# A layer kernel whose SyncE queue, norm rows, statistics and scales stand at other places of a step

## What is computed

```python
    x = L0_attn_x
    x = x + _L0_attn_ref(_layernorm(x, axis=-1), L0_attn_Wq, L0_attn_Wk, L0_attn_Wv, L0_attn_Wu, L0_attn_bu)
    x = x + _L0_ffn_ref(_layernorm(x, axis=-1), L0_ffn_W_r, L0_ffn_W_k, L0_ffn_W_v, L0_ffn_mu_r, L0_ffn_mu_k)
...
        dot = jnp.einsum('bhqd,bhkd->bhqk', q, k) / jnp.sqrt(jnp.float32(s))
        att = jax.nn.softmax(dot, axis=-1)
        out = jnp.einsum('bhqk,bhkd->bhqd', att, v)
        out = out.transpose(0, 2, 1, 3).reshape(b, t, h * s)
        return out @ Wu.T + bu
...
            xr = mu_r * x + (1.0 - mu_r) * x_prev
            xk = mu_k * x + (1.0 - mu_k) * x_prev
            r = jax.nn.sigmoid(jnp.einsum('btc,dc->btd', xr, W_r))
            k = jnp.einsum('btc,dc->btd', xk, W_k)
            k_act = jnp.square(jax.nn.relu(k))
            out = r * jnp.einsum('btc,dc->btd', k_act, W_v)
```

## Time and profile before

| | |
|---|---|
| median of 3 runs | 2272.7 us (2272.09 to 2285.43) |
| profiled execution, its own time | 2274.27 us |
| its span | 2272.4 us |
| mean granted TensorE clock | 0.972 |
| PE busy | 2114.4 us, 93% |
| DVE busy | 1872.0 us, 82% |
| ACT busy | 1645.5 us, 72% |
| POOL busy | 1514.8 us, 67% |

### The profile page before, as it was taken

The page is one execution under the profiler, slowest core; times in us unless marked ns, Lnnn a source line. Parts: engine busy times, 40 slices in busy tenths (PEclk is TensorE's granted clock), DMA queues, the critical chain, the costliest instruction groups (busy, mean ns, idle before and its releaser), DMA issues.

```text
span 2272.4 us, 39598 instructions
## 1 busy us (share of the span) xinstructions
PE 2114.4 (93%) x13084; PEld 1085.5 (48%) x13084; DVE 1872.0 (82%) x3598; ACT 1645.5 (72%) x3137; POOL 1514.8 (67%) x1568
## 2 busy tenths in 40 slices
PE   4999999999999999999999999999999999999985
PEld 3445444445454445444444544444445445454433
DVE  5788888878888888888888888888888888888762
ACT  2477777777877777777777777777777777777663
POOL 5347766667866676776676786666777667677335
PEclk8799999999999999999999999999999999999887
DMA  6544455544455553445564445555444556443410
GB/s 153 117 109 106 95 101 120 130 108 106 96 109 111 129 125 99 103 94 110 130 129 110 104 94 110 111 129 120 104 105 95 106 131 130 106 103 88 83 29 23
DMA packets 133467, 242.09 MB, mean 107 GB/s; under 512 B 24849, under 2 KB 79761, under 8 KB 120977
## 3 DMA queue, kind: packets, MB, share of 16 engines
q1 hardware_dynamic: 133264, 239.56, 47.5%
HBM read 136.71 MB, written 83.89 MB: 97 GB/s over the span
## 4 chain that ended last, share of the span: by engine, by line
PE 46%; POOL 18%; issue 15%; ACT 7%; DVE 5%; SPq 5%; DMA 4%; POOLq 0%; ACTq 0%; DVEq 0%
PE d_ps L957 19%; PE st_ps L895 12%; PE pv_ps L927 11%; PE s_ps L913 4%; SPq L314 4%; POOL parts L431 3%; DMA attnT<-attn 3%; DVE mx L707 3%; POOL xrT L440 3%; ACT yn L581 2%; ACT probs L666 2%; POOL f_lo L454 2%; POOL sums L482 2%; POOL rope_t L413 2%; POOL rope_t L416 2%
## 5 line engine op out<-in xcount | busy, mean ns | idle before, releaser
L707 DVE TENSOR_REDUCE mx<-s_ps 128x1 f32<-128x512 f32 x2048 | 1336.6, 678 | 300.9 <-PE s_ps L913 300.5
L666 ACT ACTIVATE probs<-st_ps 128x512 f32<-128x512 f32 x2048 | 1155.7, 597 | 484.9 <-PE st_ps L895 465.5
L895 PE MATMUL st_ps<-q_st,k_st 50*128 50x512 f32 x2048 | 813.3, 461 | 92.3 <-ACT probs L666 50.7
L913 PE MATMUL s_ps<-k_st,q_st 48*128 48x512 f32 x2048 | 815.8, 465 | 7.8 <-DMA k_st<-parts_scratch 5.4
L895 PEld LDWEIGHTS st_ps<-q_st,k_st 50*128 50x128 f32 x2048 | 323.2, 187 | 717.3 <-ACT probs L666 485.1
L927 PE MATMUL pv_ps<-probs,v_ext 128*32 128x512 f32 x4096 | 551.0, 610 | 0.0
L913 PEld LDWEIGHTS s_ps<-k_st,q_st 48*128 48x128 f32 x2048 | 322.6, 187 | 19.1 <-DVE mx L707 10.4
L482 POOL TENSOR_TENSOR sums<-sums,inv 128x256 f32<-128x256 f32 x128 | 93.0, 727 | 305.5 <-DVE inv L734 305.5
L461 POOL TENSOR_TENSOR f_lo<-yn,f_hi 128x512 fp32r<-128x512 f32 x128 | 166.6, 1312 | 44.8 <-ACT f_hi L631 44.7
L927 PEld LDWEIGHTS pv_ps<-probs,v_ext 128*32 128x32 f32 x4096 | 81.1, 108 | 179.1 <-issue 171.3
L431 POOL TENSOR_TENSOR parts<-parts 128x1024 fp32r<-128x1024 f32 x62 | 148.1, 2388 | 19.4 <-ACT parts L596 19.4
(11 more groups left out here) (116 smaller groups left out, 4007.2 us busy)
## 6 DMA issues: line engine op xcount, KB each, us to landing
parts_scratch<-parts SPq DMA_DIRECT2D x64, 1024.0 KB, 4.5
q_st<-parts_scratch SPq DMA_DIRECT2D x128, 256.0 KB, 5.4
k_st<-parts_scratch SPq DMA_DIRECT2D x128, 256.0 KB, 6.3
xn<-in_L_attn_x_dram SPq DMA_DIRECT2D x32, 512.0 KB, 9.2
q_st<-parts_scratch SPq DMA_DIRECT2D x128, 128.0 KB, 6.8
k_st<-parts_scratch SPq DMA_DIRECT2D x128, 128.0 KB, 7.3
attnT<-attn SPq DMA_DIRECT2D x512, 32.0 KB, 2.0
y<-in_L_attn_x_dram SPq DMA_DIRECT2D x32, 512.0 KB, 7.0
```

The source lines that it names most:

```text
L666: nc.scalar.activation(probs[:, u % SLOTS, j, :], st_ps[:, n % 2, :], ACT.Exp, scale=float(D) ** -0.5).then_inc(exp_done, 1)
L707: nc.vector.tensor_reduce(mx[:, col:col + 1], s_ps[:, ring_bank(n), :], AX.X, ALU.max).then_inc(max_done, 1)
L895: nc.tensor.matmul(st_ps[:, n % 2, :], k_st[par][row:row + SROWS + MROWS, slot, c * P:(c + 1) * P], q_st[par][row:row + SROWS + MROWS, slo ...
L913: nc.tensor.matmul(s_ps[:, ring_bank(n), :], q_st[at][row:row + SROWS, slot, qc * P:(qc + 1) * P], k_st[at][row:row + SROWS, slot, :], sta ...
```

## The change

**SyncE.** The 1 MB store of the second half of sequence b+1 stood first in the step; now the four moves of the attention result and the four of the maxima of group 1 stand before it.

**ScalarE.** The two chunks of `norm2` that ran together are made singly: at (6, 0), (6, 1), (7, 0), (7, 2) in place of two at (6, 0) and two at (7, 2). `norm1` of chunks 0 and 1 moves from (0, 0), (0, 2) of a step to (15, 0), (15, 2) of the step before (so its sequence is b+3 there), and chunks 2 and 3 from (2, 0), (2, 1) to (0, 0), (0, 2).

**VectorE.** In unit 5 the statistics of chunks 0 and 1 stand ahead of the transpose out of `pv_ps`, with both stages at place 0; the transpose and the reciprocal move to place 1. Those of chunks 2 and 3 move from (6, 1), (6, 2) to (5, 3), (6, 0).

**GpSimd.** The second norm's first `scales` stands ahead of `divide(b, 0)`. The first norm's second `scales` stands between the two pairs of rotary products of K, where it stood behind the rotary sums.

```diff
@@ SyncE's step @@
-                store_parts(b.plus(1), 1 - par, 1)
                 move_attn(b.plus(-1), 3)
                 move_max(b, 1)
+                store_parts(b.plus(1), 1 - par, 1)
                 store_out()
                 load_stacks(0)
                 load_x()
@@ GpSimd's step @@
                 low_a(1)
+                scales(b.plus(-1), 0, ln2_stat, ln2_scale, yn_done, mv2, rs2, nm2)
                 divide(b, 0)
-                for n in range(2):
-                    scales(b.plus(-1), n, ln2_stat, ln2_scale, yn_done, mv2, rs2, nm2)
+                scales(b.plus(-1), 1, ln2_stat, ln2_scale, yn_done, mv2, rs2, nm2)
...
                 rope_mults(b.plus(2), 1, 0)
+                scales(b.plus(3), 1, ln1_stat, ln1_scale, xn_done, mv1, rs1, nm1)
                 rope_mults(b.plus(2), 1, 1)
                 rope_sums(b.plus(2), 1)
-                scales(b.plus(3), 1, ln1_stat, ln1_scale, xn_done, mv1, rs1, nm1)
@@ ScalarE's step @@
-                def norm1(c):
-                    s = b.plus(2)
+                def norm1(s, c):
                     if s.active():
                         act.wait_ge(ln1_scale, s.count(6, 3 * (c // 2) + 3))
...
-                def norm2(n):
-                    s = b.plus(-1)
+                def norm2(c):
+                    s, n = b.plus(-1), c // 2
                     if s.active():
                         act.wait_ge(ln2_scale, s.count(6, 3 * n + 3))
                         if s.plus(-1).has(4, 4):
                             act.wait_ge(f_lo_done, s.plus(-1).count(4, 4))
-                        for c in (2 * n, 2 * n + 1):
-                            nc.scalar.activation(yn[:, c, :], y[1 - par][:, c, :], ACT.Identity, scale=rs2[:, c:c + 1],
-                                                 bias=nm2[:, c:c + 1]).then_inc(yn_done, 1)
+                        nc.scalar.activation(yn[:, c, :], y[1 - par][:, c, :], ACT.Identity, scale=rs2[:, c:c + 1],
+                                             bias=nm2[:, c:c + 1]).then_inc(yn_done, 1)
...
-                extras = {(0, 0): [(norm1, 0)], (0, 2): [(norm1, 1)],
+                extras = {(0, 0): [(norm1, b.plus(2), 2)], (0, 2): [(norm1, b.plus(2), 3)],
...
-                          (14, 0): [(high_f, 1, 1)], (14, 3): [(tanh, 1)]}
+                          (14, 0): [(high_f, 1, 1)], (14, 3): [(tanh, 1)], (15, 0): [(norm1, b.plus(3), 0)], (15, 2): [(norm1, b.plus(3), 1)]}
@@ VectorE's step @@
-                          (5, 0): [(normalise, b, 0, 0), (stats2_of, 0, 0)], (5, 1): [(stats2_of, 0, 1), (normalise, b, 0, 1)],
+                          (5, 0): [(stats2_of, 0, 0), (stats2_of, 0, 1)], (5, 1): [(normalise, b, 0, 0), (normalise, b, 0, 1)],
...
```

More of the change, by code:

```diff
@@ L640, in tanh @@
                                              d_ps[:, BANK["R", n], :], ACT.Tanh, scale=0.5).then_inc(tanh_done, 1)
-                extras = {(0, 0): [(norm1, 0)], (0, 2): [(norm1, 1)],
+                extras = {(0, 0): [(norm1, b.plus(2), 2)], (0, 2): [(norm1, b.plus(2), 3)],
                           (1, 2): [(high_a, 0)], (1, 3): [(v_evac, 0)],
-                          (2, 0): [(norm1, 2)], (2, 1): [(norm1, 3)], (2, 3): [(v_evac, 1)],
+                          (2, 3): [(v_evac, 1)],
                           (3, 1): [(high_a, 1)], (3, 2): [(xT_evac, 0)], (3, 3): [(xT_evac, 1)],
-                          (6, 0): [(norm2, 0)], (6, 3): [(qk_evac, 0, 0)],
-                          (7, 2): [(norm2, 1)], (7, 3): [(qk_evac, 0, 1)], (8, 2): [(yT_evac, 0)],
+                          (6, 0): [(norm2, 0)], (6, 1): [(norm2, 1)], (6, 3): [(qk_evac, 0, 0)], (7, 0): [(norm2, 2)],
+                          (7, 2): [(norm2, 3)], (7, 3): [(qk_evac, 0, 1)], (8, 2): [(yT_evac, 0)],
                           (8, 3): [(yT_evac, 1)], (9, 3): [(qk_evac, 1, 0)], (10, 0): [(high_f, 0, 0)],
@@ L836, in step @@
                           (3, 3): [(split_xnT, 0)], (4, 0): [(split_xnT, 1)], (4, 3): [(residual, 0)],
-                          (5, 0): [(normalise, b, 0, 0), (stats2_of, 0, 0)], (5, 1): [(stats2_of, 0, 1), (normalise, b, 0, 1)],
-                          (5, 2): [(residual, 1)], (5, 3): [(split_max, b, 2, 0)], (6, 0): [(split_max, b, 2, 1)],
-                          (6, 1): [(stats2_of, 1, 0)], (6, 2): [(stats2_of, 1, 1)],
+                          (5, 0): [(stats2_of, 0, 0), (stats2_of, 0, 1)], (5, 1): [(normalise, b, 0, 0), (normalise, b, 0, 1)],
+                          (5, 2): [(residual, 1)], (5, 3): [(split_max, b, 2, 0), (stats2_of, 1, 0)],
+                          (6, 0): [(split_max, b, 2, 1), (stats2_of, 1, 1)],
                           (7, 1): [(normalise, b, 0, 2)],
```

## The result

The changed kernel takes 2295.68 us (median of 20 runs, 2277.86 to 2312.21) against 2275.82 us for the kernel before (20 runs, 2267.67 to 2285.43). The ratio is 1.0088, with a 95% interval of 1.007 to 1.0106: 0.9% slower, where 2.6% faster was forecast. The slowest run, of 2312.21, was in a slower state and is left out of the ratio. The profiled execution took 2290.25 us, 16 us more than that of before.

What follows compares the result with a forecast made beforehand. TensorE is never far from busy, so time is its work plus its waits, at four places. Terms -31.9 - 13.7 + 6.2 - 14.3 - 14.9 + 5.3 + 3.3 = -60.0 gave 2213 us, 2.6% faster; range 2190 to 2250.

Steps and rivals of the forecast that it cites:

- What the store then holds up: unit 8: Loads start 2.5 us later behind the store, so unit 8's first tile waits 0.2 us a step for maxima; +6.2 us.
- The output out of the way: Output's 512 KB goes while SyncE waits for the store, so loads' start to x's landing takes 11.9 us, not 14.9.
- The maxima's own landing: Group 2's maxima, queued behind loads and x, taken as there for unit 8 when x lands, at 638.6.
- unit 4 and the long steps (units 2 to 4): Earlier maxima of group 1 save 1.03 us a step (-31.9); two thirds of long steps' 0.66 us excess returns (-13.7).
- units 5 and 6: Earlier statistics and scales gain 1.03 us a step in unit 6, less 0.55 for a late transpose; -14.3 us.
- single rows in units 7 to 9: One norm row instead of two at (7, 2) brings unit 8's second tile 0.48 us earlier a step; -14.9 us.
- row at (15, 2): The norm row moved to (15, 2), where none was, costs 0.17 us a step; +5.3 us.
- The transpose: In unit 5, moved behind statistics and a row maximum, it makes TensorE's first product wait 0.55 us a step.
- The lead-in: ScalarE's high parts of K stand behind norm rows, so the store on the chain goes later; +3.3 us, bounds 0 and 4.3.
- Rival 1: Loads lose the full 2.5 us and TensorE waits 1.3 us a step at (8, 0); +34, 2247 us, chance 0.17.
- Rival 4: Slower: store lands after 6.2 us each step, TensorE waits 3.3 us at (8, 0); +96, 2309 us, chance 0.05.
- The note that ring order speaks for rival 1 as well: Engines consume descriptors in ring order; this supports unit 4's gain and equally Rival 1, since small moves stand behind the loads.

Runs made afterwards that it cites:

- no_sp: The changed kernel with SyncE's order put back to that of the kernel before; 2259.72 us, ratio 0.9938 to the kernel before.
- out_late: The changed kernel with the output's store behind the maxima of group 3 instead of ahead of the loads; 2282.24 us, ratio 1.0058 to the kernel before.
- x_late_ts: Changed kernel, x load behind group 2's maxima, VectorE's unit 5 order restored, lead-in's K parts before norm rows, x's first statistics two places later; 2200.75 us.

## Why the prediction was wrong

**The step that failed** is "What the store then holds up: unit 8", which was +6.2 (0.2 us a step, at most 1.5). It cost 3.53 us a step. Units 7 to 9 took 2.14 us more than in no_sp in each of the first eight steps, 3.53 in the next twenty and 0.9 in step 28, 89 us in all. With that in place of 6.2 the sum is +23 us; the two medians are 20 apart. Its mechanism was named, and the loads' delay too (2.5 forecast, 2.4 in the step shown). Three numbers in it were wrong:

- *The output out of the way.* "At the same rate that is 11.9 us": the stretch took 14.9, and 14.4 before. I took one rate for all bytes, and nothing was saved. out_late shows that the output's place is worth 0.1 us of x's landing (33.62 against 33.75). x ended at 33.8, where I had 30.4 (638.6 less 608.23), and it passed my late end of 33.4 too.
- *The maxima's own landing.* I let them be there when x was. They land 0.9 us behind it.
- *The clock.* A wait of 2.26 us was followed by matmuls at half clock, 1.27 us more. The prediction counted idle time alone, and the kernel before had no such stretch in unit 8 to read it from. Its granted clock for these 20 steps, 0.99, said only that the waits in unit 4 had mostly not cost it.

**The other terms**, each per step unless said:

| | forecast | measured |
|---|---|---|
| unit 4 and the long steps (units 2 to 4) | -1.47 | -1.43 |
| units 5 and 6 | -0.46 | -0.36 |
| single rows in units 7 to 9, without the wait (no_sp) | -0.48 | -0.48 |
| row at (15, 2) | +0.17 | +0.28 |
| unit 8's maxima | +0.20 | +3.53 |

The transpose cost TensorE 0.56 us a step, as forecast (0.55). VectorE there:

```profile
633.02 0.74 DVE L754 BATCH_NORM_STATS2 stats<-y 128x6 f32<-128x256 f32 x2
633.79 0.25 DVE L761 BATCH_NORM_AGGREGATE mv<-stats 128x2 f32<-128x6 f32 x2
...
634.53 0.70 DVE L729 STREAM_TRANSPOSE sums<-pv_ps 128x512 f32<-128x512 f32 x1
```

And ScalarE's norm rows came singly with no idle time before them:

```profile
637.41 0.59 ACT L579 ACTIVATE yn<-y,nm,rs 128x256 f32<-128x256 f32 x1
...
638.38 0.60 ACT L579 ACTIVATE yn<-y,nm,rs 128x256 f32<-128x256 f32 x1
```

**The lead-in** was forecast at +3.3. The chain that ended last has the store at 38.69, 3.52 later than in the earlier trace rows, behind a row and the two parts of K:

```profile
35.27 0.60 ACT xn L570
35.87 0.52 ACT parts L594
36.88 0.53 ACT parts L594
37.43 1.24 DVE parts L826
38.69 4.27 DMA parts_scratch<-parts
```

In x_late_ts, with the parts first, it is back at 34.94:

```profile
34.94 4.30 DMA parts_scratch<-parts
```

The first exponential came 3.94 us later in the changed kernel; but out_late, with the same lead-in, has it at 77.17 and the change at 79.58, so some 2 us of such a difference vary from one execution to the next.

**The last steps** are a control that I had not thought of. In steps 29 to 31 no x is loaded: the change is 16.3 us faster there (184.6 against 200.9), 5.4 a step. That is more than the 2.0 a step that the other terms give elsewhere (1.43 + 0.36 + 0.48 - 0.28). Steps 29 and 30 of before are long (68.8 and 69.1 us from first exponential to first exponential, against 66.6 in a normal step), and those of the change get short (65.1 and 62.1); why was not tried.

**The rivals.** Rival 1 had the right mechanism and the wrong price: with the full 2.5 us of delay it gave 1.3 us a step. Rival 4 came nearest in time (2309, decided from a wait of 2.1 us), by luck, for a wrong reason: it asked for a store that lands 6.2 us after its issue, and the store took 4.4 in the step shown; of the 32 with the output behind them the latest took 5.0. I gave it 0.05, since I had closed the upper bound of the term at 1.5 by x's end and counted nothing behind it. The note that ring order speaks for rival 1 as well was the warning to follow.

What stays open: why the eight loads move bytes so much more slowly than the stores, and so why the stretch did not shrink when the output left it. Only their order was tried, not their shape, and the maxima were not tried on another engine's queue.

## What to carry to other kernels

When a large transfer is moved back in a queue, list every small transfer behind it whose reader has little slack, and take its new landing as the old one plus the whole delay, until a row shows that something shrinks. Bytes are no measure of a transfer's time when several kinds share the engines: read each kind's own GB/s. In a queue, a transfer that nobody waits for soon belongs behind the small ones that somebody does, and then its reader may have to stand a place or two later; here the first move paid in full only with the second, and the second was not tried alone. And price a long wait of TensorE above its idle time, by the granted clock in the rows behind it.

## What the hardware showed that I had not expected

- A stretch with TensorE idle for 3.2 us was followed by a granted clock of 0.50 for 3.4 us, while eight transposes took 1.97 us in place of 1.09; idle times of 0.3 us in x_late_ts, and of 1.14 us in unit 4, left it at 1.00 in the rows looked at. Over 20 steps TensorE was busy for 1309.4 us at 0.97 against 1287.6 at 0.99 for the same 8162 matmuls.
- In the changed kernel's packets the loads back from DRAM moved 178 GB/s for 16 busy engines and the 2 KB packets, for the most part of the stores, 312; slices of 0.9 us with the engines 90% busy had 364 to 382 GB/s in the store and the output, and 80 to 282 behind them.
- Taking 512 KB of output away from ahead of a busy stretch of 15 us let it end 0.1 us sooner.
